# A graph network on one core: slot products share a PSUM bank, and engines wait and signal by bank

## The chip, the cores and the metric

The kernel runs on one core of a Trainium2 chip. The metric is the device time of one execution in microseconds; lower is better. All products of 32-bit floats are made by TensorE, whose results land in PSUM, eight banks of 512 floats for each of 128 partitions.

## The reference

Four graph layers over the same graph of N = 6250 nodes and 100000 edges, which come sorted by destination. Two relational layers and two attention layers, cut to what matters:

```
h = relu(layernorm(x))
# twice (relational): sum over incoming edges, one weight matrix per edge type
W   = einsum('rb,bio->rio', w_comp, basis)               # 16 matrices 128x128
agg = segment_sum(h[src], dst*16 + type)                 # per node and type
h   = relu(einsum('nri,rio->no', agg, W) + h @ loop_w + bias)
x = x + h
h = relu(layernorm(x))
# twice (attention, 4 heads of 32): softmax over each node's incoming edges
xw = h @ W;  e = leaky_relu(al_s[src] + al_d[dst])
ee = exp(e - m[dst]);  out = segment_sum(ee/den[dst] * xw[src], dst) + b
h = elu(batchnorm(out))
x = x + h
```

## The kernel before

**Edges, tiles, windows, slots.** The sorted edges are cut into 782 tiles of 128 edges, the nodes into 49 windows of 128. A slot is a pair of a tile and a window that it touches; a tile that crosses a window's edge has two. There are 832 slots in the program (NS), so a slot's number runs ahead of its tile's by up to 48. Which slot has which tile and window is worked out on the chip in the prologue and read into registers, sixteen slots at a time.

**What a slot does.** GpSimd (POOL) gathers the 128 rows of a tile with one indirect DMA into a ring of tiles in the buffer Gr. VectorE (DVE) writes a 128x128 selection matrix (edge e goes to row d) into the ring Sr. TensorE (PE) multiplies the two into a PSUM bank, which sums the rows by destination; VectorE adds the product to the window's block of the accumulator AC. Each 32-bit product is two passes, so one slot is two MATMUL rows. SyncE (SP) turns the completion of every gather into a count that TensorE waits on (the relay). The four passes over the 832 slots are the bulk of the program; before them stand a prologue and a first transformation of all nodes.

**The relational stages (L = 0 and 1 of the first loop).** The gather ring holds TG = 64 tiles. Since the program does not know a slot's tile when it is written, the gather of tile sn waits for the product of slot sn - 16 (L1985: 64 tiles minus the 48 by which slots can be ahead); this is the count slot_products (slot_mm in the code). VectorE in its step s writes the selection of slot s + LOOK (8) and adds slot s - LAG (2) (L889, L901). TensorE's banks are RGCN_BANKS: 0, 1, 2 in the first stage, 0, 1, 2, 7 in the second, a slot to a bank, so its product of slot s waits until slot s - 3 (s - 4) is added (count slot_added). Between the slots every engine runs, from slot 96 on and for each nine slots, a *turn* that finishes one window: in L = 0 ScalarE reads the sum (L1292), TensorE turns it (L1653), VectorE copies it out (hT, L580), TensorE multiplies it with the 16 matrices of the next layer in four 512-wide products (L1675) and one more (L1677), ScalarE and VectorE evict; in L = 1 VectorE normalises (L774 to L789), ScalarE applies it (L1325), TensorE turns and projects it (L1653, L1694), ScalarE stores. All engines take the pieces of a turn in their own order of instructions, a piece for each slot.

**The attention stages (L = 0 and 1 of gat_vector and the like).** Slots go in 26 chunks of 32. While one chunk's products are made and added (TensorE L1896, VectorE L1088, banks 0 and 1, a slot to a bank), a generator named prep prepares the weights of the next chunk in pieces that all engines take between their slots: for the first twelve slots of a chunk selections, casts, transposes and small products (VectorE L986, ScalarE L1471 and L1479, TensorE L1824 and L1838), and from slot 14 on, every second slot, a chain that goes to and fro between VectorE, ScalarE and TensorE (scans, column maxima, exponentials). Three times in a chunk VectorE multiplies eight slots' rows with their weights (L1062). ScalarE also copies every slot's rows from the gather ring of RT = 32 tiles to its place (L1447); the gather of tile t waits until all slots of tile t - 32 are copied, a count that SyncE passes on from ScalarE to GpSimd (L2034, L2002).

The four waits that the change touches are, in TensorE and VectorE: 

```
if s >= len(banks): e.wait_ge(slot_add, L * NS + s - len(banks) + 1)      # TensorE, relational
e.wait_ge(slot_mm, L * NS + sa + 1)                                       # VectorE, relational
if s >= 2: e.wait_ge(gat_add, L * NS + s - 1)                             # TensorE, attention
e.wait_ge(gat_mm, L * NS + s + 1)                                         # VectorE, attention
```

## Time and profile before

| | |
|---|---|
| time, median of 3 runs | 5923.72 us (5916.72 to 5936.73) |
| the profiled execution | 5916.48 us, of which the span from first to last instruction is 5914.7 us |
| first relational stage, first to last add | 292.7 to 1537.2 us |
| second relational stage | 1564.2 to 2750.4 us |
| first attention stage | 2879.3 to 4272.7 us |
| second attention stage | 4438 to 5867 us (window used) |

The profile gives busy time of each engine, the idle time before each instruction and what ended it (the releaser). "issue" is a wait for nothing that the profile shows, "remote" is a releaser that it could not name. Starts of TensorE's rows are when the instruction was let go, their ends are modelled; the moment at which VectorE starts an add that waited shows when the product's signal was there. Loads of registers from memory and waits alone are not counted as busy.

### The profile page before, as it was taken

To read this page: it belongs to the slowest core of one execution; us is meant where nothing else is said; L and a number is where in the kernel's file an instruction comes from. 1 tells how busy PE (TensorE), PEld (TensorE's weight loads), DVE (VectorE), ACT (ScalarE), POOL (GpSimd) and SP (SyncE) were. 2 spreads that over 40 slices of the span, in tenths; PEclk is the share of its full clock that TensorE was granted. 3 is DMA by queue.
4 is the path that set the end of the run, shared out by engine and by line. 5 is a ranking of instruction groups with operands and counts; after the bars stand their busy time and mean duration, and the time that the engine had idled before them with its cause. 6 is when DMAs were issued, how large, how long until landed. Compare 5 with 4: busy or idle time off the path is not lost.

```text
span 5914.7 us, 74475 instructions
## 1 busy us (share of the span) xinstructions
PE 3344.7 (57%) x13433; PEld 2400.5 (41%) x13433; DVE 2636.7 (45%) x10097; ACT 1461.1 (25%) x4313; POOL 3023.1 (51%) x3161
## 2 busy tenths in 40 slices
PE   6946666666544444444355556666625555566566
PEld 2433334344333333333234434544514444454454
DVE  5433333333334444444344445555634444455556
ACT  2301111111100000001323323333233333333333
POOL 0066666665366666664555554555155554544540
PEclk8957777777655555555555555556655555555555
DMA  5513333333312222221111111111021111111111
GB/s 207 229 45 115 122 122 123 117 120 125 102 50 55 56 55 55 55 55 37 41 41 39 37 38 36 36 39 38 8 56 41 38 37 35 38 36 36 37 35 45
DMA packets 167180, 389.46 MB, mean 66 GB/s; under 512 B 57159, under 2 KB 92549, under 8 KB 149446
## 3 DMA queue, kind: packets, MB, share of 16 engines
q0 software_dynamic: 100096, 208.40, 14.7%
q10 hardware_dynamic: 39116, 105.76, 4.8%
q1 hardware_dynamic: 27514, 70.51, 3.2%
q8 instruction: 131, 2.15, 0.1%
q14 instruction: 323, 2.65, 0.1%
HBM read 223.09 MB, written 161.35 MB: 65 GB/s over the span
## 4 chain that ended last, share of the span: by engine, by line
PE 33%; another core or an unknown queue 21%; issue 19%; DVE 16%; ACT 4%; DVEq 3%; DMA 1%; ACTq 1%; POOL 1%; SPq 0%; POOLq 0%
PE B L1896 9%; PE B L1769 8%; PE B L1675 5%; DVE AC L901 3%; DVE AC L1088 3%; PE B L1736 3%; DVE Sr L986 2%; PE B L1838 2%; PE B L1824 2%; DVEq L323 1%; DVE Sr L889 1%; POOL Gr L1986 1%; ACT Gr L1447 1%; DVE Gr L1062 1%
## 5 line engine op out<-in xcount | busy, mean ns | idle before, releaser
L2004 POOL DMA_INDIRECT Gr<-Gtab,SRC x1564 | 1513.5, 968 | 1488.1 <-SPq L2034 905.0
L1986 POOL DMA_INDIRECT Gr<-Ttab,GID x1564 | 1485.2, 950 | 1033.1 <-issue 406.7
L1896 PE MATMUL B<-Gr,Sr 128*128 128x136 f32 x3328 | 1187.6, 476 | 945.1 <-DVE AC L1088 503.1
L1769 PE MATMUL B<-Gr,Sr 128*128 x3328 | 919.9, 403 | 710.4 <-issue 369.6
L1896 PEld LDWEIGHTS B<-Gr,Sr 128*128 128x128 f32 x3328 | 808.2, 304 | 1176.6 <-DVE AC L1088 618.4
L1769 PEld LDWEIGHTS B<-Gr,Sr 128*128 128x128 f32 x3328 | 743.3, 280 | 1081.1 <-issue 1077.4
L1088 DVE TENSOR_TENSOR AC<-AC,B 128x136 f32 x1664 | 486.9, 293 | 1192.6 <-remote 599.0
L901 DVE TENSOR_TENSOR AC<-AC,B 128x128 f32 x1664 | 476.0, 286 | 927.6 <-remote 427.8
L889 DVE TENSOR_SCALAR Sr<-iota,DL 128x128 f32<-128x128 f32 x1664 | 497.2, 301 | 15.6 <-issue 10.8
L1675 PE MATMUL B<-XW,hT 128*128 128x512 f32 x672 | 455.8, 769 | 73.9 <-issue 38.4
L1447 ACT COPY Gr<-Gr 128x132 f32 x1664 | 422.7, 301 | 265.5 <-issue 132.7
L1824 PE MATMUL B<-identb,hold 128*128 128x128 bf16 x1664 | 251.9, 304 | 237.4 <-ACT hold L1479 124.5
L1471 ACT CAST hold<-Sr 128x512 bf16<-128x512 f32 x416 | 257.8, 620 | 487.6 <-DVE Sr L986 365.6
L986 DVE TENSOR_SCALAR Sr<-iota,DL 128x128 f32<-128x128 f32 x1664 | 363.8, 287 | 0.1
L1300 ACT COPY Sr<-B 128x512 f32<-128x512 f32 x336 | 196.0, 587 | 625.0 <-PE B L1675 355.0
L1824 PEld LDWEIGHTS B<-identb,hold 128*128 128x128 bf16 x1664 | 188.6, 140 | 280.7 <-ACT hold L1479 143.8
L1479 ACT COPY hold<-B 128x512 bf16<-128x512 bf16 x416 | 244.1, 587 | 111.9 <-PE B L1838 47.8
L1062 DVE TENSOR_TENSOR Gr<-Gr,B 128x1024 f32<-128x1024 f32 x202 | 245.3, 1214 | 1.3 <-issue 0.6
L1838 PE MATMUL B<-A,hold 128*128 x1664 | 164.0, 185 | 60.4 <-ACT hold L1479 28.2
L580 DVE COPY hT<-B 128x128 f32<-128x128 f32 x217 | 62.6, 289 | 295.4 <-remote 182.2
L1838 PEld LDWEIGHTS B<-A,hold 128*128 128x128 bf16 x1664 | 147.9, 118 | 108.4 <-issue 92.6
L1736 PE MATMUL B<-XW,hT 128*128 128x512 f32 x392 | 181.2, 606 | 3.8 <-DVE hT L580 3.8
(275 smaller groups left out, 2928.0 us busy)
## 6 DMA issues: line engine op xcount, KB each, us to landing
Ttab<-Sr ACTq DMA_DIRECT2D x84, 1024.0 KB
Ttab<-Sr SPq DMA_DIRECT2D x51, 1024.0 KB
Gr<-Ttab,GID POOLq DMA_INDIRECT x1564
Gr<-Gtab,SRC POOLq DMA_INDIRECT x1564
Gtab<-Gr ACTq DMA_DIRECT2D x84, 66.0 KB
X1D<-Gr ACTq DMA_DIRECT2D x84, 64.0 KB
Gtab<-XW SPq DMA_DIRECT2D x7, 462.0 KB, 3.4
out<-Sr SPq DMA_DIRECT2D x12, 256.0 KB
```

The source lines that it names most:

```text
L889: e.tensor_scalar(out=selr(sn), in0=iota[:, :], scalar1=DL[:, sn:sn + 1], scalar2=None, op0=ALU.is_equal).then_inc(built_v, 1)
L901: e.tensor_tensor(a, a, B[RGCN_BANKS[L][sa % len(RGCN_BANKS[L])]][:, 0:P], ALU.add).then_inc(slot_add, 1)
L986: e.tensor_scalar(out=sel(s), in0=iota[:, :], scalar1=DL[:, s:s + 1], scalar2=None, op0=ALU.is_equal).then_inc(sel_made, 1)
L1088: e.tensor_tensor(a, a, B[s % 2][:, 0:CW], ALU.add).then_inc(gat_add, 1)
L1447: e.copy(Gr[:, (s % GR) * CW:(s % GR) * CW + 132], Gr[:, bass.ds(o + RB, 132)]).then_inc(copied[L], 1)
L1675: e.matmul(B[bk][:, :], hT[:, u % 2, :], wl[1][:, i * 512:(i + 1) * 512], start=True, stop=True).then_inc(row_mm, 1)
L1769: e.matmul(B[banks[s % len(banks)]][:, 0:P], selr(s), Gr[:, bass.ds(o, P)], start=True, stop=True).then_inc(slot_mm, 1)
L1824: mm = e.transpose(bt[:, j * P:(j + 1) * P], sbf[:, g % 2, j * P:(j + 1) * P], identb[:, :])
L1838: mm = e.matmul(B[5][:, 12 * m:12 * m + 12], sts[:, g % 2, j * P:(j + 1) * P], A3[:, bass.ds(off(e, regs[m % 16], 12 * NW), 12)], start=Tr ...
L1896: e.matmul(B[s % 2][:, 0:CW], sel(s), Gr[:, (s % GR) * CW:(s % GR + 1) * CW], start=True, stop=True).then_inc(gat_mm, 1)
L1986: e.indirect_dma_start(out=Gr[:, (sn + 1) % TG * P:((sn + 1) % TG + 1) * P], out_offset=None, in_=Tt[L][:, :], in_offset=bass.IndirectOffs ...
L2004: e.indirect_dma_start(out=Gr[:, o:o + 132], out_offset=None, in_=T2[L][0:NPAD][:, :], in_offset=bass.IndirectOffsetOnAxis(ap=SRC[:, t:t + ...
```

## The change

In the relational stages four slots share a bank (banks 0, 1, 2 in both): TensorE waits for the adds of the bank's last use, for the selections and for the tile of the bank's last slot once for four slots, and signals once, with the fourth product. VectorE waits once for four slots and adds one by one as before; its LAG becomes 5. GpSimd's wait for slot sn - 16 becomes one for the bank that holds it. In the attention stages eight slots go as three, three and two in banks 0 and 1 in turn, VectorE's lag stays 2 (GLAG); ScalarE copies rows in fours behind one wait and one signal, and SyncE frees the ring by four tiles. What is multiplied, gathered, copied and added, and in which order, is unchanged.

```diff
-LOOK, LAG = 8, 2
+LOOK, LAG, GLAG = 8, 5, 2
+Q = 4
-RGCN_BANKS = ((0, 1, 2), (0, 1, 2, 7))
+RGCN_BANKS = (0, 1, 2)
+def batch_of(s):
+
+    j = min(s % 8 // 3, 2)
+    return 3 * (s // 8) + j, s // 8 * 8 + 3 * j, s // 8 * 8 + (3, 6, 8)[j]
+        def product(s):
+            return B[RGCN_BANKS[s // Q % len(RGCN_BANKS)]][:, s % Q * P:(s % Q + 1) * P]
+        def attended(s):
+            b, first, _ = batch_of(s)
+            return B[b % 2][:, (s - first) * CW:(s - first + 1) * CW]
...
-                        e.wait_ge(slot_mm, L * NS + sa + 1)
+                        if sa % Q == 0:
+                            e.wait_ge(slot_mm, (L * NS + sa) // Q + 1)
-                        e.tensor_tensor(a, a, B[RGCN_BANKS[L][sa % len(RGCN_BANKS[L])]][:, 0:P], ALU.add).then_inc(slot_add, 1)
+                        e.tensor_tensor(a, a, product(sa), ALU.add).then_inc(slot_add, 1)
...
-                e.wait_ge(gat_mm, L * NS + s + 1)
+                b, first, _ = batch_of(s)
+                if s == first:
+                    e.wait_ge(gat_mm, L * NBATCH + b + 1)
...
-                while at[0] < min(c * CH + n, NS):
+                while at[0] + Q <= min(c * CH + n, NS):
-                    e.wait_ge(landed[2 + L], tr[s % 16])
+                    e.wait_ge(landed[2 + L], tr[s % 16 + Q - 1])
+                    for s in range(s, s + Q):
...
-                        if s >= len(banks):
-                            e.wait_ge(slot_add, L * NS + s - len(banks) + 1)
-                        else:
-                            e.wait_ge(built_v, L * NS + s + 1)
-                        e.wait_ge(landed[L], kregs[s % 32 // 16][s % 16])
+                        if s % Q == 0:
+                            if s // Q >= len(RGCN_BANKS):
+                                e.wait_ge(slot_add, L * NS + s + Q - Q * len(RGCN_BANKS))
+                            else:
+                                e.wait_ge(built_v, L * NS + s + Q)
+                            e.wait_ge(landed[L], kregs[s % 32 // 16][s % 16 + Q - 1])
+                        mm = e.matmul(product(s), selr(s), Gr[:, bass.ds(o, P)], start=True, stop=True)
+                        if s % Q == Q - 1:
+                            mm.then_inc(slot_mm, 1)
...
-                    if s >= 2:
-                        e.wait_ge(gat_add, L * NS + s - 1)
+                    _, first, end = batch_of(s)
+                    if s == first and s >= 6:
+                        e.wait_ge(gat_add, L * NS + batch_of(batch_of(first - 1)[1] - 1)[2])
+                    mm = e.matmul(attended(s), sel(s), Gr[:, (s % GR) * CW:(s % GR + 1) * CW], start=True, stop=True)
+                    if s + 1 == end:
+                        mm.then_inc(gat_mm, 1)
...
-                        e.wait_ge(slot_mm, L * NS + back + 1)
+                        e.wait_ge(slot_mm, (L * NS + back) // Q + 1)
...
-                    if t >= RT:
-                        e.wait_ge(freed[L], t - RT + 1)
+                    if t >= RT and t % Q == 0:
+                        e.wait_ge(freed[L], t - RT + Q)
...
-                    e.wait_ge(copied[L], lregs[u % 16])
-                    e.sem_inc(freed[L], 1)
+                    if u % Q == Q - 1:
+                        e.wait_ge(copied[L], lregs[u % 16])
+                        e.sem_inc(freed[L], Q)
```

TensorE's instructions at the start of the first relational stage, before. B0 to B2 are the banks; landed0 counts tiles, slot_added counts adds.

```order
L323 ISA [waits landed0,slot_added]
L1769 MATMUL B0<-Gr,Sr 128x128
L323 ISA [waits landed0,slot_added]
L1769 MATMUL B1<-Gr,Sr 128x128
L323 ISA [waits landed0,slot_added]
L1769 MATMUL B2<-Gr,Sr 128x128
L323 ISA [waits landed0,slot_added]
L1769 MATMUL B0<-Gr,Sr 128x128
```

The same place in the changed kernel:

```order
L340 ISA [waits landed0,slot_added]
L1796 MATMUL B0<-Gr,Sr 128x128
L340 ISA
L1796 MATMUL B0<-Gr,Sr 128x128
L340 ISA
L1796 MATMUL B0<-Gr,Sr 128x128
L340 ISA
L1796 MATMUL B0<-Gr,Sr 128x128
L340 ISA [waits landed0,slot_added]
L1796 MATMUL B1<-Gr,Sr 128x128
```

No product moved against another; the two waits stand before the first of four products, and the bank changes with them.

VectorE's instructions in the attention stage, slots 14 to 18 of a chunk, before (SB, ST and CC belong to the chain of prep; gat_products counts products, gat_added adds):

```order
L1088 TENSOR_TENSOR AC<-AC,B1 128x136
L1067 TENSOR_LOAD OFF
L323 ISA [waits gat_added,gat_products]
L1088 TENSOR_TENSOR AC<-AC,B0 128x136
L1006 SCALAR_TENSOR_TENSOR hold<-pen,hold 128x128 [waits prep_vector]
L323 ISA [waits gat_added,gat_products]
L1088 TENSOR_TENSOR AC<-AC,B1 128x136
L1062 TENSOR_TENSOR Gr<-Gr,B6 128x8x128 [waits prep_scalar]
L323 ISA [waits gat_added,gat_products]
L1088 TENSOR_TENSOR AC<-AC,B0 128x136
L1012 SCALAR_TENSOR_TENSOR SB<-PB,FF 1x132 [waits prep_scalar]
```

and in the changed kernel:

```order
L1113 TENSOR_TENSOR AC<-AC,B1 128x136
L1089 TENSOR_LOAD OFF
L1113 ISA [waits gat_products,gat_added]
L1113 TENSOR_TENSOR AC<-AC,B0 128x136
L1028 SCALAR_TENSOR_TENSOR hold<-pen,hold 128x128 [waits prep_vector]
L1113 ISA [waits gat_added]
L1113 TENSOR_TENSOR AC<-AC,B0 128x136
L1084 TENSOR_TENSOR Gr<-Gr,B6 128x8x128 [waits prep_scalar]
L1113 ISA [waits gat_added]
L1113 TENSOR_TENSOR AC<-AC,B0 128x136
L1034 SCALAR_TENSOR_TENSOR SB<-PB,FF 1x132 [waits prep_scalar]
```

The order is the same. The first of the three adds now waits for the products of all three slots, ahead of the scan L1028; the other two wait only for the add before them.

## Rows read from the trace of the kernel before

**Rows 1.** The page: span, busy time, granted clock in 40 slices.

```profile
span 5914.7 us, 74475 instructions
PE 3344.7 (57%) x13433; PEld 2400.5 (41%) x13433; DVE 2636.7 (45%) x10097; ACT 1461.1 (25%) x4313; POOL 3023.1 (51%) x3161
PEclk8957777777655555555555555556655555555555
```

**Rows 2.** Windows of the four slot stages: busy time, granted clock, DMA share.

```profile
core 0: us, PE busy (x) PEld busy (x) DVE busy (x) ACT busy (x) POOL busy (x), PEclk, DMA share, GB/s
292.00:1538.00 1246.00, 804.85 (x2591) 488.51 (x2591) 456.41 (x1830) 220.03 (x420) 740.81 (x780) 0.75 0.33 110
1553.00:2751.00 1198.00, 557.05 (x1910) 435.13 (x1910) 497.38 (x2240) 93.56 (x328) 741.70 (x782) 0.53 0.21 55
2879.00:4274.00 1395.00, 829.34 (x3943) 647.60 (x3943) 714.62 (x2654) 478.70 (x1570) 682.19 (x711) 0.55 0.16 35
4438.00:5867.00 1429.00, 844.85 (x3943) 662.61 (x3943) 713.73 (x2655) 479.35 (x1570) 681.92 (x711) 0.53 0.15 35
```

**Rows 3.** Waits of GpSimd, first relational stage: us, times, longest.

```profile
POOL Gr L1986 <- PE B L1769: 137.3, 143, 2.6
POOL Gr L1986 <- remote: 86.8, 46, 4.8
```

**Rows 4.** Waits of GpSimd, second relational stage.

```profile
POOL Gr L1986 <- remote: 153.2, 79, 3.4
POOL Gr L1986 <- PE B L1769: 50.8, 76, 5.1
```

**Rows 5.** Timeline of VectorE, second relational stage, slots 8 to 14.

```profile
1573.34 0.29 DVE L901 TENSOR_TENSOR AC<-AC,B 128x128 f32 x1 [3.00 <-remote]
...
1578.94 0.29 DVE L901 TENSOR_TENSOR AC<-AC,B 128x128 f32 x1 [5.11 <-remote]
...
1583.85 0.29 DVE L901 TENSOR_TENSOR AC<-AC,B 128x128 f32 x1 [4.43 <-remote]
...
1588.75 0.29 DVE L901 TENSOR_TENSOR AC<-AC,B 128x128 f32 x1 [4.42 <-remote]
...
1591.57 0.29 DVE L901 TENSOR_TENSOR AC<-AC,B 128x128 f32 x1 [2.33 <-remote]
...
1592.06 0.29 DVE L901 TENSOR_TENSOR AC<-AC,B 128x128 f32 x1
```

**Rows 6.** Timeline of TensorE over the same stretch.

```profile
1568.81 2.86 PE L1769 MATMUL B<-Gr,Sr 128*128 x10 [0.55 <-issue]
1573.76 0.79 PE L1769 MATMUL B<-Gr,Sr 128*128 x2 [2.09 <-issue]
1579.36 0.79 PE L1769 MATMUL B<-Gr,Sr 128*128 x2 [4.81 <-issue]
```

**Rows 7.** Timeline of GpSimd over the same stretch.

```profile
1584.35 0.95 POOL L1986 DMA_INDIRECT Gr<-Ttab,GID  x1 [0.30 <-issue]
1585.60 0.94 POOL L1986 DMA_INDIRECT Gr<-Ttab,GID  x1 [0.30 <-issue]
1589.38 0.94 POOL L1986 DMA_INDIRECT Gr<-Ttab,GID  x1 [2.84 <-remote]
```

**Rows 8.** Waits over the whole run: the turns' copies out and projections.

```profile
PE B L1694 <- DVE hT L580: 112.2, 20, 9.6
DVE hT L580 <- remote: 182.2, 38, 10.9
```

**Rows 9.** Groups of TensorE in the first relational stage: busy, mean ns, idle before.

```profile
L1675 PE MATMUL B<-XW,hT 128*128 128x512 f32 x656 | 448.2, 773 | 73.3 <-issue 38.4 <-ACT Sr L1300 20.4 <-DVE hT L580 11.9
```

**Rows 10.** Groups of VectorE, first attention stage.

```profile
L1088 DVE TENSOR_TENSOR AC<-AC,B 128x136 f32 x832 | 243.5, 293 | 569.4 <-remote 271.6 <-PE B L1896 196.9 <-issue 68.0
```

**Rows 11.** Waits of GpSimd for the ring, first and second attention stage.

```profile
POOL Gr L2004 <- SPq L2034: 427.2, 144, 9.8
POOL Gr L2004 <- SPq L2034: 457.2, 138, 10.1
```

**Rows 12.** Timeline of VectorE in an attention chunk, and of TensorE behind it.

```profile
3312.86 0.29 DVE L1088 TENSOR_TENSOR AC<-AC,B 128x136 f32 x1 [3.69 <-remote]
3316.40 0.30 DVE L1088 TENSOR_TENSOR AC<-AC,B 128x136 f32 x1 [3.25 <-remote]
3319.57 3.45 PE L1896 MATMUL B<-Gr,Sr 128*128 128x136 f32 x10 [1.99 <-DVE AC L1088]
```

More of the change, by code:

```diff
@@ L62 @@
 MIXV = counted("mkb mkh w0 c0 wdg0 w1 c1 wdg1")
-TABV = counted("dF sF gF tF lF wf0 wf1 wff nwc cin rs ce cei cs wb cemax " + " ".join(f"sel{b} pm{b}" for b in range(TPR)) +
+TABV = counted("dF sF gF tF lF wf0 wf1 wff nwc cin rs ce cei1 cei cs wb cemax " + " ".join(f"sel{b} pm{b}" for b in range(TPR)) +
                " ti0 th0 tl0 lb gid slh slk sli slb wbi wbs wb2 wbf wb2l il0 dl0 il1 dl1 ofs0 ofs1"
@@ L617, in tables_vector @@
             after("ce")
-            then(e.tensor_copy(cei, ce), "cei")
+            then(e.tensor_scalar(out=cei, in0=ce, scalar1=float(Q - 1), scalar2=None, op0=ALU.add), "cei1")
+            after("cei1")
+            then(e.tensor_scalar(out=cei, in0=cei, scalar1=2, scalar2=None, op0=ALU.arith_shift_right), "cei")
             then(e.tensor_tensor(cs, ce, nwc, ALU.subtract), "cs")
@@ L894, in vector @@
                             e.reg_load(vregs[sa % 32 // 16], OFF[0:1, sa:sa + 16])
-                        e.wait_ge(slot_mm, L * NS + sa + 1)
+                        if sa % Q == 0:
+                            e.wait_ge(slot_mm, (L * NS + sa) // Q + 1)
+                        o = off(e, vregs[sa % 32 // 16][sa % 16], NW * CW)
                         e.wait_ge(slot_add, L * NS + sa)
@@ L899, in vector @@
                             vpos["self"] = 0
[L900 to L901 removed]
+                        a = AC[:, bass.ds(o, P)]
+                        e.tensor_tensor(a, a, product(sa), ALU.add).then_inc(slot_add, 1)
                         vpos["add"] = L * NS + sa + 1
@@ L1081, in add @@
                     e.wait_ge(gat_scale, 2 * t + 2)
-                e.wait_ge(gat_mm, L * NS + s + 1)
+                b, first, _ = batch_of(s)
+                if s == first:
+                    e.wait_ge(gat_mm, L * NBATCH + b + 1)
+                o = off(e, regs[s % 16], NW * CW)
                 e.wait_ge(gat_add, L * NS + s)
@@ L1086, in add @@
                     done[1] = 0
-                a = AC[:, bass.ds(off(e, regs[s % 16], NW * CW), CW)]
-                e.tensor_tensor(a, a, B[s % 2][:, 0:CW], ALU.add).then_inc(gat_add, 1)
+                a = AC[:, bass.ds(o, CW)]
+                e.tensor_tensor(a, a, attended(s), ALU.add).then_inc(gat_add, 1)
             den, mmx = acw[:, 0:NW, 128:132], acw[:, 0:NW, 132:136]
@@ L1171, in gat_vector @@
                         weigh(c, i // 8 + 1)
-                    if s >= LAG:
-                        add(s - LAG)
-                        done[0] = s - LAG + 1
+                    if s >= GLAG:
+                        add(s - GLAG)
+                        done[0] = s - GLAG + 1
                     if i < 12 or (i >= 14 and i % 2 == 0):
@@ L1188, in gat_vector @@
                     weigh(c + 1, 0)
-            for s in range(NS - LAG, NS):
+            for s in range(NS - GLAG, NS):
                 add(s)
@@ L1442, in copies @@
                     if s >= GR:
-                        e.wait_ge(gat_mm, L * NS + s - GR + 1)
-                    e.wait_ge(landed[2 + L], tr[s % 16])
-                    o = off(e, rr[s % 16], (RT - 1) * 132)
-                    e.copy(Gr[:, (s % GR) * CW:(s % GR) * CW + 132], Gr[:, bass.ds(o + RB, 132)]).then_inc(copied[L], 1)
-                    at[0] += 1
+                        e.wait_ge(gat_mm, L * NBATCH + batch_of(s + Q - 1 - GR)[0] + 1)
+                    e.wait_ge(landed[2 + L], tr[s % 16 + Q - 1])
+                    for s in range(s, s + Q):
+                        o = off(e, rr[s % 16], (RT - 1) * 132)
+                        ins = e.copy(Gr[:, (s % GR) * CW:(s % GR) * CW + 132], Gr[:, bass.ds(o + RB, 132)])
+                    ins.then_inc(copied[L], 1)
+                    at[0] += Q
             def prep(c):
@@ L1745, in tensor @@
                 turn = iter(())
-                banks = RGCN_BANKS[L]
                 def start(k):
```

16 lines of the change are left out of this document (7 added, 9 removed).

## The prediction

> **What bounds the kernel now.** I read the page first: no engine is busy for more than 57% of the span [rows 1], so waits set the time. The windows of the four slot stages come next [rows 2]: 1246, 1198, 1395 and 1429 us, 5268 of 5915 us, with the clock granted to TensorE at 0.75 in the first and 0.53 to 0.55 (the 1.2 GHz level for nearly all of the time) in the others. The rest of the program is not touched.
>
> In a relational stage GpSimd has the firmest floor. Undisturbed it starts a gather each 1.25 us, 0.95 busy and 0.30 of issue [rows 7], and 782 tiles x 1.25 = 978 us. Its waits for slot_products are 137.3 + 86.8 = 224.1 us in the first stage [rows 3] and 153.2 + 50.8 = 204.0 us in the second [rows 4]; 1246 - 224 = 1022 and 1198 - 204 = 994 us, close to the floor. ("remote" at L1986 can only be the same semaphore or the gather queue's own completion; I take it for the first, since it ends in step with VectorE's late adds.)
>
> Why is a product late, when TensorE is busy for 557 of 1198 us? The timelines show it. VectorE's adds, 0.29 us each, come at 1573.3, 1578.9, 1583.9 and 1588.8, each after 3 to 5 us of idling, and then two more at once [rows 5]; TensorE, behind, is let go for one slot (two rows) at a time, 4.8 us apart [rows 6], and GpSimd is then held for 2.84 us [rows 7]. An add waits for a product's signal, and the product four slots on waits for that add: with only three or four slots open, a delay of one signal is paid again at each slot. What delays the first signal the trace does not show. With twelve slots open the loop should be paid once for four slots, and GpSimd is 16 slots off, so it sees less of it.
>
> The turns are the second chain: projections wait up to 9.6 us for hT, and VectorE's copies of hT wait 182.2 us in 38 waits [rows 8]; in the first stage the four wide products of all turns alone take 448.2 us of TensorE, in order between the slots [rows 9]. The change leaves this chain alone.
>
> In the attention stages GpSimd is held by the ring instead, 427.2 and 457.2 us [rows 11]: copies, products and adds are all late together. VectorE idles 569.4 us of the first one ahead of its adds [rows 10], 3.69 and 3.25 us before single ones, and TensorE behind it waits 1.99 us for an add before ten rows go in 3.45 us [rows 12]. Part of this is the two-bank handshake, which the change relaxes, and part is prep's chain between three engines, which it doesn't.
>
> **The change part by part.**
>
> 1. First relational stage, banks of four and 12 slots open instead of 3. The gain lies between 0 and GpSimd's 224.1 us [rows 3]. TensorE has work for 805 of 1246 us [rows 2] and its turns stay serial [rows 9], so not all is freed; with TensorE free to run ahead more than half should be. I take 0.6: -134.5 us.
> 2. Second relational stage, 12 open instead of 4. Between 0 and 204.0 us [rows 4]. TensorE has only 557 us of work here [rows 2], nearly all hold-ups look like those of [rows 5], and turns cost VectorE and TensorE little. I take 0.8: -163.2 us.
> 3. LAG 5 and the wait for a whole bank: the first add of a bank waits for three more products, at most 4 x 0.79 = 3.2 us of TensorE's rows [rows 6]. It comes three steps later too, and the turns' pieces stand behind it on VectorE, which in turn let TensorE go on. Taken at nothing, since VectorE is busy for only 456 and 497 us [rows 2]; without that cover it is the part of the 224 and 204 us that I leave in. GpSimd's wait for a bank costs at most 3 of its 16 slots of lead, 3 x 1.25 = 3.8 us, once a stage if it is never held up again: nothing.
> 4. Attention, three, three and two slots: five or six slots open instead of two. The nearest row of what it could free is GpSimd's wait, 427.2 + 457.2 = 884.4 us [rows 11]; the bounds are 0 and that. TensorE is held by the handshake, but prep's chain sets the pace from slot 14 on in every chunk of 32, and VectorE's idling [rows 10] is shared between the two. Nearer the low end: 0.2, -176.9 us.
> 5. VectorE's first add of an attention batch stands with GLAG 2 in the step of the batch's last product (the last but one step before). It waits for all of it, and the scans L1028, L1034 of prep are queued behind; on them ScalarE and TensorE wait. A slot's two rows take 3.45 / 5 = 0.69 us [rows 12]. A batch of three waits for two more slots and one of two for one more: 5 x 0.69 = 3.45 us for eight slots, 208 times, 718 us if all is exposed. It is covered where TensorE runs ahead, which it may now, and I have put the rest into the 0.2 of step 4.
> 6. ScalarE's copies in fours, SyncE's frees by four, selections signalled in fours: a tile's place comes free up to 3 x 1.25 = 3.8 us later, with 32 places. Nothing while the whole stage is slower than GpSimd's pace (1395 / 782 = 1.78 us a tile); if the attention stages came down to that pace it would cost up to this much at each hold-up. Two more small operations in the prologue: below 1 us.
> 7. Fewer signals: 416 + 624 = 1040 product signals instead of 3328. The trace has no price for one; it lies inside steps 1, 2 and 4.
>
> The sum is -134.5 - 163.2 - 176.9 = -474.6 us. The profiled execution took 5916.5, so the changed one 5441.9; the median stands 7.2 above the profiled one, and so I predict 5450 us.
>
> The Trainium skill speaks against the change in "PSUM — Partial Sum Buffer", section "PSUM bank collisions raise a hardware error": engines must be kept apart by bank and quarter of the partitions, not by address, so neighbouring slots in one bank can't be written and read in turn. Adds then have to wait for the whole bank, which is the 718 us of step 5 if nothing covered it; no run here shows a collision.
>
> **The rivals.**
>
> A, my forecast, **62%**: 5450. Its own bounds: 0.4 of 428.1 and 0.1 of 884.4 give 259.7 (5657 + 7 = 5664); 0.85 and 0.3 give 629.2 (5294).
>
> B, the turns and prep's chain rule, **16%**: hold-ups end later because hT and the turns' products are late [rows 8, 9], not because of the window. For it speaks that a late first signal has no cause in the trace. Against it: in [rows 5] no turn is running (they begin at slot 96). A quarter of the relational waits, 107 us, and nothing in attention: 5917 - 107 + 7 = 5817.
>
> C, attention is freed too, **11%**: TensorE's waits for adds were the root, 0.9 x 428.1 + 0.5 x 884.4 = 827.5: 5096. For it speaks 569 us of VectorE's idling before adds [rows 10]; against it, that granted clock and turns stay.
>
> D, slower, **8%**: the wait for a whole bank in attention (step 5) holds up the scans and so ScalarE and TensorE, a loop of its own in each batch. It decides once it is exposed for more than 298 / 718 = 41% with nothing won from step 4. At 70%: 5917 + 503 - 298 + 7 = 6129. For it: the add of a batch stands in the very step of the batch's last product. Against it: before, each slot waited 1.99 us on an add [rows 12], and this is gone.
>
> E, it does nothing, **3%**: signals are late for a reason that neither number nor depth touches: 5924.
>
> On the price of signals the Trainium skill has a figure, "TensorE: Matmul & The Clock Gate", section "The cost: per-tile semaphore tail": increments at the end of matmuls queue up at 26.3 ns each. By that page alone an estimate is 2288 x 26.3 ns = 60 us saved at most, so about 5864; the 2.3 to 5 us waits of [rows 5] are a hundred times larger, and no rule for one increment explains them.
>
> **How the numbers follow.** A and B reach from 5280 to 5860 and hold 78%, with the near edges of the others 80%; that is the range. Faster by over 0.3% (18 us, about what a measurement of this kernel can tell from no change) are A, B and C, 89%; within it E, 3%; slower D, 8%.
>
> **What would show it.** Step 1 and 2: GpSimd's waits at the gathers below 90 and 45 us, stages of about 1110 and 1035 us, TensorE in groups of eight rows of slots, no run of adds 4.9 us apart. Step 3: VectorE's waits ahead of each fourth add only, and no longer in sum. Step 4: attention windows near 1310 and 1340 us, GpSimd's ring waits about 340 and 370. Step 5: if wrong, VectorE's idling before first adds grows beyond 569 us and ScalarE's waits for the scans with it. Wrong would be above all: hold-ups of the gathers that stay with 12 slots open (B), or attention stages that don't move or grow (D).

## The result and the profile after

The changed kernel took 5949.03 us (median of 6 runs, 5945.01 to 5958.99), the kernel before in the same comparison 5923.97 us: ratio 1.0047, interval 1.0025 to 1.0069. It is slower by 25 us where 474 us less was forecast. Its profiled execution took 5945.55 us, with a span of 5943.8 us.

One thing has to be said ahead of the experiments, since their numbers can't be read without it: in different sets of runs the kernel before took either 5919 to 5956 us, as in the first measurement, or 4636 to 4638 us, each steadily. I call them the **5.9 ms sets** and the **4.6 ms sets**. The kernel, the input and the work are the same, and two chip numbers each stand in a set of each kind, so the number doesn't tell which it will be. Every ratio below is against the kernel before in the same set.

The windows of the four stages, changed kernel (the rows that answer to [rows 2]):

```profile
core 0: us, PE busy (x) PEld busy (x) DVE busy (x) ACT busy (x) POOL busy (x), PEclk, DMA share, GB/s
298.00:1549.00 1251.00, 745.20 (x2586) 455.99 (x2585) 414.94 (x1827) 220.14 (x420) 735.84 (x776) 0.74 0.33 109
1576.00:2766.00 1190.00, 460.74 (x1904) 400.54 (x1903) 464.32 (x2228) 93.40 (x328) 731.79 (x772) 0.56 0.20 53
2892.00:4313.00 1421.00, 759.68 (x3929) 630.19 (x3929) 704.80 (x2652) 474.95 (x1563) 681.48 (x712) 0.54 0.15 35
4477.00:5896.00 1419.00, 756.27 (x3929) 627.74 (x3929) 705.66 (x2652) 475.08 (x1563) 679.65 (x711) 0.55 0.15 35
```

From first to last add the stages last 1249.3, 1187.9, 1418.8 and 1417.1 us, against 1244.5, 1186.2, 1393.4 and 1427.2 before. The 29 us between the two spans are 5.9 ahead of the first add, 7.6 in the relational stages and the gaps behind them, and 15.6 in attention and what follows it. TensorE's rows did get denser (its busy time in the second stage falls from 557 to 461 us, since the modelled ends of back-to-back rows overlap), and nothing came of it.

GpSimd's waits in the two relational stages, changed kernel (against [rows 3, 4]):

```profile
POOL Gr L2018 <- remote: 121.2, 43, 4.5
POOL Gr L2018 <- PE B L1796: 95.7, 51, 6.2
...
POOL Gr L2018 <- remote: 150.8, 50, 4.9
POOL Gr L2018 <- PE B L1796: 41.8, 15, 5.3
```

216.9 and 192.6 us, against 224.1 and 204.0: with twelve slots open instead of three or four GpSimd is held as long as ever. Three timelines of the second stage show how. TensorE, changed kernel:

```profile
1625.77 2.07 PE L1796 MATMUL B<-Gr,Sr 128*128 x8 [2.94 <-SPq L2052]
1630.65 2.07 PE L1796 MATMUL B<-Gr,Sr 128*128 x8 [2.81 <-SPq L2052]
1635.73 2.07 PE L1796 MATMUL B<-Gr,Sr 128*128 x8 [3.01 <-issue]
1640.64 2.07 PE L1796 MATMUL B<-Gr,Sr 128*128 x8 [2.84 <-issue]
1649.92 2.07 PE L1796 MATMUL B<-Gr,Sr 128*128 x8 [7.21 <-DVE AC L923]
```

VectorE, the adds of the banks multiplied at 1625.8, 1630.7 and 1635.7:

```profile
1637.62 0.29 DVE L923 TENSOR_TENSOR AC<-AC,B 128x128 f32 x1 [12.81 <-remote]
1638.09 0.28 DVE L923 TENSOR_TENSOR AC<-AC,B 128x128 f32 x1
...
1648.21 0.29 DVE L923 TENSOR_TENSOR AC<-AC,B 128x128 f32 x1 [8.80 <-remote]
...
1650.86 0.29 DVE L923 TENSOR_TENSOR AC<-AC,B 128x128 f32 x1 [0.91 <-issue]
```

and GpSimd:

```profile
1642.91 0.95 POOL L2018 DMA_INDIRECT Gr<-Ttab,GID  x1 [0.30 <-issue]
1648.77 0.95 POOL L2018 DMA_INDIRECT Gr<-Ttab,GID  x1 [4.91 <-remote]
```

TensorE keeps up with the gathers, a bank each 5 us, as hoped. But the bank of 1630.7 is added at 1648.2, some 16 us after its last row, and the next two banks' signals are there by then too. Meanwhile GpSimd has used up its lead, stands still from 1643.9, and only then do the signals arrive. The trace also holds the updates of the count slot_products itself, and they agree: for these four banks they stand at 1637.4, 1648.0, 1648.1 and 1648.2 us, so it isn't VectorE that looks late. VectorE's own signals are prompt: the fourth add of the bank ends at 1649.76, and TensorE's wait for it ends at 1649.82. What the trace can't tell is whether the product is late or only its signal, since the ends of TensorE's rows are modelled. The delay is not made by the window; the window only decides how many products it covers.

In the kernel before, the traces show the same thing from GpSimd's side. In its second stage, by the updates that the trace kept, three or more product signals come within 0.5 us of each other 46 times, and each time GpSimd stands still for more than 1 us at that moment or did in the 5 us ahead of it, which is so for only 43% of the stage. In the first stage it is 26 times out of 26, against 52%. By itself this doesn't say which is the cause, since missing signals also make GpSimd stop; the longer lead and the stage without gathers below do.

The attention stages, first one: VectorE's adds and TensorE's products, changed kernel (VectorE against [rows 10]):

```profile
L1113 DVE TENSOR_TENSOR AC<-AC,B 128x136 f32 x832 | 241.4, 290 | 670.8 <-remote 287.1 <-PE B L1926 183.3 <-issue 163.4
L1926 PE MATMUL B<-Gr,Sr 128*128 128x136 f32 x1654 | 502.2, 449 | 163.0 <-DVE AC L1113 68.8 <-issue 47.3 <-DVE Gr L1084 46.5
```

The row of TensorE's products in the kernel before:

```profile
L1896 PE MATMUL B<-Gr,Sr 128*128 128x136 f32 x1660 | 587.5, 472 | 451.4 <-DVE AC L1088 253.1 <-issue 192.8 <-DVE Gr L1062 1.5
```

VectorE now idles 670.8 us ahead of its adds, 101 more than before; TensorE's waits for them fall from 253.1 to 68.8 us. GpSimd's waits for the ring in the two stages (against [rows 11]) are as long in sum but twice as long at the longest, 20 us:

```profile
POOL Gr L2036 <- SPq L2067: 438.1, 91, 20.5
...
POOL Gr L2036 <- SPq L2067: 436.9, 91, 20.2
```

### The profile page after: what moved, and what is told of

The parts are those of the page before. It is cut to its first block, busy times and chain, and to the rows that moved or that the text cites. A ratio compares the mean times of both kernels' runs of the same rounds, so it can differ in the third digit from the quotient of the medians.

```text
span 5943.8 us, 69987 instructions
## 1 busy us (share of the span) xinstructions
PE 3040.8 (51%) x13433; PEld 2289.1 (39%) x13433; DVE 2546.6 (43%) x10098; ACT 1454.7 (24%) x4313; POOL 3018.3 (51%) x3161
## 4 chain that ended last, share of the span: by engine, by line
issue 24%; another core or an unknown queue 22%; PE 21%; DVE 18%; ACT 5%; DVEq 3%; POOL 3%; ACTq 2%; DMA 1%; POOLq 0%; SPq 0%
PE B L1926 5%; PE B L1702 5%; DVE AC L1113 4%; DVE AC L923 3%; PE B L1763 3%; DVE Sr L1008 3%; POOL Gr L2018 3%; DVE Sr L908 2%; PE B L1796 2%; ACT hold L1506 1%; ACT Gr L1473 1%; ACT hold L1498 1%; PE B L587 1%; PE B L1680 1%
## 5 line engine op out<-in xcount | busy, mean ns | idle before, releaser
L1926 PE MATMUL B<-Gr,Sr 128*128 128x136 f32 x3328 | 1007.3, 448 | 327.9 <-DVE AC L1113 143.1
L1926 PEld LDWEIGHTS B<-Gr,Sr 128*128 128x128 f32 x3328 | 781.4, 313 | 385.3 <-DVE AC L1113 161.2
L1796 PEld LDWEIGHTS B<-Gr,Sr 128*128 128x128 f32 x3328 | 681.7, 278 | 577.7 <-issue 576.8
L1796 PE MATMUL B<-Gr,Sr 128*128 x3328 | 739.2, 371 | 311.1 <-issue 131.3
L1702 PE MATMUL B<-XW,hT 128*128 128x512 f32 x672 | 475.3, 800 | 95.6 <-DVE hT L597 38.7
L1473 ACT COPY Gr<-Gr 128x132 f32 x1664 | 373.0, 298 | 266.0 <-issue 183.7
L1680 PE MATMUL B<-ident,hn 128*128 128x128 f32 x217 | 85.0, 393 | 559.0 <-issue 194.8
L1853 PEld LDWEIGHTS B<-identb,hold 128*128 128x128 bf16 x1664 | 165.2, 133 | 477.1 <-ACT hold L1506 284.0
L1680 PEld LDWEIGHTS B<-ident,hn 128*128 128x128 f32 x217 | 34.8, 161 | 603.4 <-issue 214.2
L777 DVE TENSOR_TENSOR AC<-B,rb 128x128 f32 x84 | 24.5, 291 | 490.1 <-PE B L1704 247.2
```

Of the source, the lines that this page charges most:

```text
L1473: ins = e.copy(Gr[:, (s % GR) * CW:(s % GR) * CW + 132], Gr[:, bass.ds(o + RB, 132)])
L1702: e.matmul(B[bk][:, :], hT[:, u % 2, :], wl[1][:, i * 512:(i + 1) * 512], start=True, stop=True).then_inc(row_mm, 1)
L1796: mm = e.matmul(product(s), selr(s), Gr[:, bass.ds(o, P)], start=True, stop=True)
L1853: mm = e.transpose(bt[:, j * P:(j + 1) * P], sbf[:, g % 2, j * P:(j + 1) * P], identb[:, :])
L1926: mm = e.matmul(attended(s), sel(s), Gr[:, (s % GR) * CW:(s % GR + 1) * CW], start=True, stop=True)
```

## The experiments

**The two parts apart** (a 4.6 ms set, the kernel before 4635.64 us). `rel_only` is the kernel before with the relational hunks of the diff, `att_only` with the attention hunks.

> The relational part of the change alone (four slots to a bank, LAG 5), attention as before. In the changed kernel's trace the two relational stages lasted 1249.3 and 1187.9 us against 1244.5 and 1186.2 before, so if the stages are what they seem this stands within 15 us of the kernel before (ratio 0.999 to 1.003). Rival: the relational part gains and the attention part loses it again in a way that the stage lengths hide; then this would be over 0.5% faster than before.

> The attention part of the change alone (three, three and two slots to a bank, copies and frees by four), relational stages as before. The two attention stages lasted 1418.8 and 1417.1 us in the changed kernel against 1393.4 and 1427.2 before: +15 us. If the batch costs what it seems, this is 10 to 25 us slower than before (ratio 1.002 to 1.004), and the same kernel as the changed one in its time. Rival: the whole +25 us is the prologue's and relational part's, and this is within 5 us of before.

Measured: `rel_only` 4642.19 us, ratio 1.0016 (1.0007 to 1.0025). `att_only` 4773.17 us, 1.0297 (1.0283 to 1.0311). The relational part costs 7 us; of these 5 are that the first add now waits for a whole bank (it comes at 298.3 us, against 293.3 in `lead_before` of the same set). The attention part costs 137 us here, far above what I expected: its stages take 1116 and 1114 us against 1043 and 1046 in `lead_before` of the same set.

**A longer lead for GpSimd.** CROSS is the list of the 48 tiles at which a window changes.

```diff
-                    back = sn - TG + NS - NT
-                    if back >= 0:
-                        e.wait_ge(slot_mm, L * NS + back + 1)
+                    if sn >= TG:
+                        e.wait_ge(slot_mm, L * NS + slots_to(sn - TG))
```

> The kernel before, with GpSimd's wait at a gather of a relational stage on the last slot of the tile whose place it takes, by a list of the tiles at which a window changes, instead of on slot sn - 16: a lead of up to 63 slots at the stage's start, down to 16 at its end. Theory 'ring lead': products are signalled up to 17 us late in stretches, whatever the window of TensorE, and only GpSimd's lead of 16 slots (20 us at 1.25 us) decides what of this is lost; the stages fall towards 782 x 1.25 = 978 us, by 100 us or more each, 200 to 350 us in all. Rival 'the window after all': the holds stay 4.9 us for each slot with three or four slots open, TensorE and VectorE set the pace, under 60 us in all.

> The changed kernel with the same longer lead of GpSimd. Theory 'ring lead': with twelve slots open and the lead no longer binding, the stages come to 1000 to 1080 us each, 250 to 350 us faster than before, and at least as fast as the kernel before with the longer lead. Rival 'turns': the windows' turns (one for nine slots, serial between three engines) set the pace of 1.43 to 1.5 us a slot and it gains under 60 us.

In this 4.6 ms set `lead_before` took 4635.8 us, ratio 0.9999 (0.999 to 1.0008), and `lead_after` 4772.11 us, 1.0297, which is the attention part's loss alone. The lead is worth nothing here because there is nothing to win; `lead_before`'s relational windows:

```profile
293.00:1297.00 1004.00, 753.31 (x2589) 452.04 (x2588) 456.38 (x1830) 220.38 (x420) 737.18 (x779) 0.80 0.41 136
1323.00:2295.00 972.00, 649.10 (x1910) 452.78 (x1909) 506.19 (x2227) 92.99 (x326) 731.13 (x774) 0.50 0.25 65
```

972 us for 782 gathers is GpSimd's own pace of 1.25 us each. In a 4.6 ms set signals are not held: in the second stage of `lead_before` 7 of 832 adds start more than 3 us after their product's second row, the latest after 3.6 us, where in the kernel before of the first measurement 370 do. In `glag4` (below), whose relational part is the changed kernel's, VectorE adds each bank 0.6 us after the start of its last row (TensorE's groups of eight rows start there at 1346.32, 1351.23 and 1356.30):

```profile
1348.61 0.29 DVE L923 TENSOR_TENSOR AC<-AC,B 128x128 f32 x1 [3.25 <-PE B L1796]
...
1353.52 0.29 DVE L923 TENSOR_TENSOR AC<-AC,B 128x128 f32 x1 [3.17 <-PE B L1796]
...
1358.59 0.29 DVE L923 TENSOR_TENSOR AC<-AC,B 128x128 f32 x1 [3.32 <-PE B L1796]
```

The same kernel in a 5.9 ms set (before 5956.01 us):

> The kernel before with GpSimd's lead up to 63 slots, again, for the case that this chip is of the kind of the first measurement. Theory 'ring lead': the holds of the product signals last up to 17 us, and a lead of 16 slots (20 us) is what loses them; the relational stages get 50 us or more shorter each, most where the lead is longest (the first 113 slots have 63). Rival 'the loop of three and four slots': TensorE waits for adds that wait for late signals, and the lead changes under 20 us in each stage. On the other kind of chip it changes nothing, as it did.

5982.13 us, ratio 1.0041 (1.0025 to 1.0058): slower, so "ring lead" is refuted. The first stage takes 1283.7 us against 1259.3 in `dry_before_b` of the same set, whose first stage is that of the kernel before, so the lead changes a little more than the rival's 20 us, and for the worse. What the trace shows at the start of its second stage is the mechanism in its purest form. VectorE:

```profile
1646.67 0.29 DVE L908 TENSOR_TENSOR AC<-AC,B 128x128 f32 x1 [5.11 <-issue]
1652.28 0.29 DVE L908 TENSOR_TENSOR AC<-AC,B 128x128 f32 x1 [5.12 <-remote]
...
1697.22 0.29 DVE L908 TENSOR_TENSOR AC<-AC,B 128x128 f32 x1 [5.15 <-remote]
```

GpSimd, whose gathers ran at 1.25 us up to here:

```profile
1709.07 0.95 POOL L1992 DMA_INDIRECT Gr<-Ttab,GID  x1 [4.07 <-remote]
```

As long as GpSimd has room, it gathers, and just as long every product is signalled late, one in 5.6 us with four slots open. The first 100 slots of the stage take 222 us, against 151 in the kernel before of the first measurement. The first stage is the same: the longest time from a product's second row to its add, among the first sixty slots, is 35 us here and 19 us with a lead of 16. The longer the lead, the longer the stretch.

**No gathers, other DMAs.** `dry_before` and `dry_after` leave out the gathers of the second relational stage; `probe_plain` replaces them by plain DMAs of SyncE, of the same 64 KB:

```diff
+                    if t >= 16:
+                        e.wait_ge(slot_mm, L * NS + t - 15)
+                    r = t % 384 * P
+                    e.dma_start(Gr[:, (t + 1) % TG * P:((t + 1) % TG + 1) * P], Tt[1][r:r + P, :]).then_inc(plain[t % 16], 16)
```

> The kernel before with no gathers in the second relational stage (products read what the ring holds, so that stage's values mean nothing; the rest is as it was). It shows how long TensorE, VectorE and ScalarE need for the stage without GpSimd. If the window of four slots had cost anything with gathers, this stage now lasts 700 us or more; theory 'gathers rule': it takes well under 974 us, 600 to 850, set by the adds and the turns.

> The changed kernel with no gathers in the second relational stage. What the bank of four is worth where no gather is waited for is the difference to the same run of the kernel before: theory 'worth it, but hidden': 50 to 250 us shorter than there. Rival 'turns': within 30 us, as the turns' chain is the same.

> The kernel before without gathers in the second relational stage, again, for a chip of the kind of the first measurement. If the late product signals come with gathers in flight, the stage now takes about 654 us, as on the other kind. If they are TensorE's own, it takes 900 us or more, with adds 4 to 5 us apart in stretches.

> The kernel before, but in the second relational stage SyncE moves each tile in with one plain DMA of 64 KB instead of GpSimd's gather of 128 rows (other rows of the same table, so that stage's values mean nothing); same ring, same wait for slot sn - 16. For a chip where the kernel before takes over 5900 us. With no gathers at all that stage took 653 us there and its products were signalled in time. Theory 'gathers by GpSimd': only DMAs that GpSimd makes hold TensorE's signals back, and the stage takes under 1000 us with signals in time. Rival 'any DMA into the ring': signals come late in stretches again, 1100 us or more. On the other kind of chip only the first holds.

Measured, second stage from first to last add, one execution each. In a 4.6 ms set: before 653.8, changed 597.9 us. In 5.9 ms sets: `dry_before_b` 653.0 us, `probe_plain` 655.4 us. The windows of `dry_after`, `dry_before_b` and `probe_plain`:

```profile
1322.00:1921.00 599.00, 397.48 (x1905) 348.76 (x1903) 454.95 (x2224) 93.13 (x328) 0.00 (x0) 0.70 0.07 20
```

```profile
1580.00:2233.00 653.00, 482.61 (x1907) 395.05 (x1906) 483.33 (x2227) 93.30 (x328) 0.00 (x0) 0.64 0.07 19
```

```profile
1577.00:2233.00 656.00, 483.33 (x1907) 394.56 (x1906) 483.67 (x2228) 93.39 (x328) 0.00 (x0) 0.64 0.34 95
```

So TensorE and VectorE do the whole stage in 653 us in either kind of set, and half of the adds come within 1.7 us of the start of their product's second row; more than 3 us after it come 16 and 19 adds in the two 5.9 ms runs, against 370 of 832 with gathers. Plain transfers into the ring, which bring the stage's DMA traffic from 19 to 95 GB/s, do not disturb them; GpSimd's gathers at 53 to 55 GB/s in all do. It isn't the number of packets either. The queue that fills the ring, from 1600 to 2200 us, in `probe_plain` and then in the kernel before (packets, MB, share of the DMA engines; the first also carries other plain transfers):

```profile
q1 hardware_dynamic: 105243, 47.94, 29.2%
```

```profile
q0 software_dynamic: 13056, 26.76, 17.5%
```

The plain DMAs differ from gathers in more than who makes them (they read rows that lie together, and GpSimd does nothing in the stage), so which part of a gather does it stays open. And the bank of four, with its LAG of 5, is worth 56 us of this stage, but only where nobody waits for a gather: "worth it, but hidden" holds, just inside its 50 to 250 us.

> The kernel before with two probes: in the first relational stage GpSimd's lead is 8 slots instead of 16, in the second each gather moves half a row (256 bytes for each of the 128 rows, so that stage's values mean nothing). For a chip where the kernel before takes over 5900 us. Theory 'gathers hold the signals, and GpSimd's stop lets them go': with a lead of 8 GpSimd stops sooner and more often, holds are shorter (at most 8 slots), and the stage's length is within 5% of before (1244 us). Rival 'lead is lost time': 1350 us or more. Second stage: if the bytes hold the signals back, it gets shorter by 50 us or more (1186 us before); if the number of gathers or descriptors does, it stays within 30 us.

Its edits are `back = sn - TG + NS - NT + 8` in the first stage, and in the second the table seen as half rows. In the 5.9 ms set of before 5918.88 us the stages took 1238.5 and 1193.0 us (1244.5 and 1186.2 in the first measurement): neither half the lead nor half the bytes changes the length, in one execution. With lead 8 the longest delay among the first sixty slots of the first stage is 13 us, with lead 16 it was 19. GpSimd is held about as often and as long, 183 times and 234 us against 189 and 224, so shorter holds did not come with more stops, as the theory had it.

**The changed kernel again, and the shared banks alone** (a 5.9 ms set, before 5927.23 us). `banks_alone` is the changed kernel with copies, frees and selection signals by one, as before:

```diff
-                    e.wait_ge(landed[2 + L], tr[s % 16 + Q - 1])
-                    for s in range(s, s + Q):
-                        o = off(e, rr[s % 16], (RT - 1) * 132)
...
-                    ins.then_inc(copied[L], 1)
+                    e.wait_ge(landed[2 + L], tr[s % 16])
+                    o = off(e, rr[s % 16], (RT - 1) * 132)
...
-                    if u % Q == Q - 1:
-                        e.wait_ge(copied[L], lregs[u % 16])
-                        e.sem_inc(freed[L], Q)
+                    e.wait_ge(copied[L], lregs[u % 16])
+                    e.sem_inc(freed[L], 1)
```

> The changed kernel itself, once more. On the chip of the first measurement it took 5949.0 us against 5924.0 us. If this chip is like the two of the experiments so far (the kernel before at 4636 to 4638 us, products signalled 0.6 us after they start), it is 2.6 to 3.3% slower than before, as its attention part alone was (ratio 1.0297). If this chip is like the first one (before at 5924 us), the ratio is 1.002 to 1.007 again.

> The changed kernel with ScalarE's copies, SyncE's frees and VectorE's selection signals by one tile or slot as before: of the attention part only the shared banks (three, three and two) stay. The copies by four alone cost 73 us (ratio 1.0156), the whole attention part 137 us. Theory 'two costs that add': this costs about 65 us with the relational part's 7 (ratio 1.012 to 1.018). Rival 'one chain': both hold up the same chain, so that the banks alone already cost 100 us or more (ratio above 1.022).

`after_again`: 5955.16 us, 1.0044 (1.0029 to 1.006), the first result once more. `banks_alone`: 5867.02 us, **0.9888** (0.9857 to 0.9919): both of my readings foresaw a loss, since they came from a 4.6 ms set, and it beats both kernels. It was repeated twice in other 5.9 ms sets:

> The shared banks without the copies by four, on this chip. On the kind of the first measurement: ratio 0.985 to 0.993 again. On the kind where the kernel before takes 4636 us: by theory 'two costs that add' 1.012 to 1.018, by 'one chain' above 1.022, and under 1.005 if only the copies by four cost anything.

> The shared banks without the copies by four. Where the kernel before takes over 5900 us: ratio 0.988 to 0.996 a third time. Where it takes 4636 us: by 'two costs that add' 1.012 to 1.018, by 'one chain' above 1.022, under 1.005 if only the copies by four cost anything there.

5920.87 us against 5956.01, 0.9949 (0.9931 to 0.9968), and 5858.8 us against 5918.88, 0.9898 (0.9877 to 0.9919). The attention stages of `banks_alone` take 1368 to 1394 us in the three sets, those of the changed kernel in the 5.9 ms sets 1417 to 1432.

**What costs what in attention, 4.6 ms sets.** `copies_by_four` is the kernel before with nothing but the copies, frees and selection signals by four, `att_banks` with nothing but the shared banks; `glag4` is the changed kernel with `GLAG = 4` and the steps after a window's end moved by two with it; `banks_glag4` has the shared banks, GLAG 4 and copies by one.

> The kernel before with ScalarE's copies, SyncE's frees and VectorE's selection signals by four alone; products and adds go by one slot. Theory 'batch wait': within 10 us of before. Rival 'copies by four': 70 us slower in each attention stage.

> The kernel before with the shared banks of the attention stages (three, three and two slots) and nothing else of the change. Where the kernel before takes over 5900 us: the banks with the relational part gave ratios 0.9888, 0.9949 and 0.9898, and the relational part showed 6 to 7 us of loss, so 0.987 to 0.994. Where it takes 4636 us: the copies by four alone cost 73 us and the whole attention part 137 us; by 'two costs that add' 1.010 to 1.017, by 'one chain' above 1.022, under 1.003 if only the copies by four cost anything there.

> The changed kernel with GLAG 4 instead of 2 (adds of the attention stages two steps later, and the work after a window's end with them), so that VectorE's first add of a batch of three has the two steps between it and the batch's last product that every add had before. Theory 'batch wait': the loss of the attention part, 70 us for each stage on the chip of the first four runs, is VectorE's first add waiting in the very step of the last product; with GLAG 4 both stages come back to within 15 us of the kernel before. Rival 'copies by four': the loss comes from ScalarE's copies or SyncE's frees, and GLAG changes under 10 us of it.

> Shared banks with copies, frees and selection signals by one, and GLAG 4. On a chip where the kernel before takes 5924 us the banks alone were 1.1% faster; theory 'batch wait': the first add's wait still costs there, and this is another 0.3 to 1% faster (ratio 0.978 to 0.986). On a chip where the kernel before takes 4636 us all four stages stand at GpSimd's pace of 1.25 us a gather already, and this is within 0.4% of before. Rival: adds two steps later hold back TensorE's banks and the ring's places as much as they save, ratio 0.988 or above on the first kind.

Measured: `copies_by_four` 4710.33 us, 1.0156 (1.0139 to 1.0173); `att_banks` 4691.92 us, 1.0118 (1.0101 to 1.0135); `glag4` 4639.88 us, 1.0002 (0.9992 to 1.0012). 72 and 56 us are 128 of the 137 that both together cost: two costs that nearly add. For `copies_by_four` neither reading was right: 72 us is far above the 10 of "batch wait", and half of the 70 us in each stage of its rival. `copies_by_four` has copies, frees and selection signals by four together; which of the three costs was not run. VectorE's adds in the first attention stage show it too; `rel_only` (attention as before):

```profile
L1094 DVE TENSOR_TENSOR AC<-AC,B 128x136 f32 x832 | 241.0, 290 | 229.3 <-PE B L1905 187.4 <-DVE AC L1094 30.4 <-issue 3.3
```

`copies_by_four`, then `att_banks`:

```profile
L1107 DVE TENSOR_TENSOR AC<-AC,B 128x136 f32 x832 | 241.5, 290 | 279.4 <-PE B L1917 239.1 <-DVE AC L1107 17.2 <-DVE AC L1096 6.0
```

```profile
L1106 DVE TENSOR_TENSOR AC<-AC,B 128x136 f32 x832 | 241.9, 291 | 323.8 <-PE B L1914 264.6 <-DVE AC L1106 17.7 <-issue 7.3
```

`att_only`, then `glag4`:

```profile
L1108 DVE TENSOR_TENSOR AC<-AC,B 128x136 f32 x832 | 241.2, 290 | 367.6 <-PE B L1918 311.0 <-DVE AC L1108 16.2 <-issue 5.5
```

```profile
L1113 DVE TENSOR_TENSOR AC<-AC,B 128x136 f32 x832 | 241.5, 290 | 198.2 <-PE B L1926 146.5 <-DVE AC L1102 6.0 <-DVE AC L1113 5.0
```

Read the first number behind the second bar: 229 us of idling ahead of the adds before, 279 with copies by four, 324 with the banks, 368 with both, and 198 once each add stands two steps further from its bank's last product. With that the first attention stage is back at 1042.5 us (1041.7 in `rel_only`), although copies still go by four: the two steps cover both costs. That the copies' cost is covered too was not expected.

`banks_glag4` ran in the 5.9 ms set of before 5956.01 us: 5890.28 us, 0.9907 (0.988 to 0.9934). In the same set `banks_alone_b` had 0.9949, so the two steps are worth another 31 us there, in the one set that has both (four runs each, which do not overlap). "Batch wait" foresaw 0.978 to 0.986 from the level of 0.9888; the step has the size foretold, but the ratio itself lies where the rival was put, at 0.988 or above, since `banks_alone_b` had less to start from.

## Why the prediction was wrong

**What bounds the kernel.** Right that GpSimd's 978 us is the floor of a relational stage: the 4.6 ms sets stand on it (971 to 1010 us). Right too that late product signals are what keeps the stages above it. The step that failed is the next: *"with twelve slots open the loop should be paid once for four slots, and GpSimd is 16 slots off, so it sees less of it."* This took the delay of a signal as given and asked only how often it is paid. I had written that the trace does not show what delays the first signal, and gave 62% to a mechanism that needed it to be independent of GpSimd. The runs show that it isn't: no gathers, no delay (653 us); other DMAs, no delay (655 us); gathers with more room, a longer delay (up to 35 us instead of 19, and 222 us for 100 slots). The reading that fits all of this is a loop: in a 5.9 ms set GpSimd gathers until missing signals stop it, its stop lets them through, and it starts again. The measured pace is 1.43 to 1.54 us a slot whether 3, 4 or 12 slots are open and whether the lead is 8, 16 or up to 63.

**Steps 1 and 2**, -134.5 and -163.2 us: measured +4.8 and +1.7. The bound of nothing, which each step had, was the value.

**Step 3**, nothing: measured 5 of the 7 us of `rel_only`, at the kernel's first add, which waits for a whole bank with no other work beside it.

**Step 4**, -176.9 us with bounds of 0 and 884: the sign was right for the 5.9 ms sets and the size was not. The shared banks with copies by one, relational part included, gave -60, -35 and -60 us; in a 4.6 ms set they cost 56 us in `att_banks`. In the changed kernel TensorE idles only 163 us ahead of its products in the first attention stage, instead of 451, but VectorE's idling grew from 569 to 671 us. The handshake had been where TensorE waited, not what set the stage's length.

**Step 5**, put into the 0.2 of step 4: it is a cost of its own. `att_banks` shows 56 us (of the 718 us bound, 8%), less whatever step 4 gave back there, which no run separates, and two steps of GLAG take it away.

**Step 6**, nothing "while the whole stage is slower than GpSimd's pace": wrong, and what turned the sign. In the 5.9 ms set of `after_again`, with attention at 1.8 us a tile, the changed kernel stands 88 us above `banks_alone`. By itself it cost 72 us in a 4.6 ms set; there a stage of 1043 us is 1.33 us a tile, near GpSimd's 1.25, and the step's own reservation (up to 3.8 us at each hold-up at that pace) does allow a cost, and GpSimd's longest wait for the ring in the first attention stage grows from 5.4 us in `rel_only` to 9.6 us. I had priced the copies by four only through the ring's places and GpSimd. ScalarE also has the casts and copies of prep in the same queue: a wait for the fourth tile and four copies in a row stand ahead of them, and VectorE's and TensorE's steps behind those. That this is the way the loss takes is read from VectorE's idling, not tried by itself; what is shown is that copies, frees and selection signals by four cause it together.

**Step 7**, fewer signals: 1248 fewer in the relational stages, and these took 4.8 and 1.7 us more. No saving shows.

**Rivals.** The final number lies in none. E (3%) is nearest in time, and its "signals are late for a reason that neither number nor depth touches" is what the relational stages showed; it was the rival to which I gave least. D (8%) had part of the mechanism in attention, the wait for a whole bank, but not the copies by four, and its loss of 205 us is eight times too large for the first measurement. B doubted the window too, with the wrong reason, the turns: late signals stand ahead of the first turn and vanish where the turns stay but the gathers don't (653 us).

**The sum, redone:** +6 at the first add and +7.5 in the relational part (first measurement), and in attention -73 for the banks (the -60 us of `banks_alone` less these 13) and +88 for the copies by four (`after_again` less `banks_alone`): 28 us. The last two come from one set and add up by themselves to the 28 us that `after_again` lost there, so this divides the loss and doesn't check it; the first measurement had 25 us.

**Open:** what part of the machine holds the signals back, and why only in some sets of runs. It takes GpSimd's gathers; it isn't their bytes, and it isn't any DMA. Their number per time was not varied by itself, and the runs without gathers are one execution each. No run leaves out the gathers of an attention stage: there too adds come late in the 5.9 ms sets (170 of 832 more than 3 us after their product's second row in the kernel before, 29 in `lead_before`), but that this makes the 350 to 380 us by which these stages are longer is not shown. Neither `banks_glag4` in a 4.6 ms set nor `glag4` in a 5.9 ms set was run. Of what was run, the shared banks with copies by one are best in the 5.9 ms sets, and better with GLAG 4 (5890.28 us) than with 2 (5920.87 us) in the one set that has both; in the 4.6 ms sets nothing beats the kernel before.

## What to carry to other kernels

Before pricing a deeper window, ask who makes the delay that it is to hide. If the engine that the window frees feeds the delay (here GpSimd, whose gathers hold back the signals that its own next gathers wait for), the loop can regulate itself, and the window then moves nothing; taking the feeder out of one stage is the quickest test. Where copies, waits or signals are put together by four, look at everything else in that engine's queue, not only at the buffer that comes free later, and when adds are put together by bank, move them back as well (here by two steps, for banks of three).

## What the runs showed of the hardware

The same kernel took 4636 us or 5924 us in different sets of runs, with the same duration of each gather (0.95 us), of each add (0.29 us) and about the same granted clock (0.50 to 0.56 in the second stage). In the relational stages the difference is in when TensorE's signals arrive. With gathers in flight in the 5.9 ms sets they come up to 19 us after the row that carries them (up to 35 us with the long lead), several at once around GpSimd's stops. Without gathers, or with plain DMAs from SyncE instead (95 GB/s in all), half of the adds start within 1.7 us of that row and none later than 3.9 us. In the 4.6 ms sets, with gathers, half start within 0.6 us of it in the second stage. The rule of the Trainium skill, "PSUM — Partial Sum Buffer", section "PSUM bank collisions raise a hardware error", to guard PSUM by bank, is kept by every kernel here; no run breaks it. Where three slots share a bank, so that the first add waits in the step of the bank's last product, the kernel is 56 us of 4636 slower (`att_banks`), and once the adds stand two steps later nothing is left that can be measured (`glag4`, ratio 1.0002).
